# A third token buffer, a second stacked buffer, norms in four pieces, a late merge inside a pair, and inverses by block transposes, in an attention-plus-FFN kernel on one Trainium2 core

## The reference

```python
x = x + attn(layernorm(x), ctx, mask)      # LN of x again inside attn, with g1, b1; LN of ctx with g2, b2
#   q = xn @ Wq.T; k = cn @ Wk.T; v = cn @ Wv.T      (16 heads of 32)
#   softmax(q k^T / sqrt(32), masked) @ v, then @ Wo.T + bo
x = x + ffn(layernorm(x))                   # ffn: rows and weight quantised to fp6 (e2m3) with a
#   scale per block of 32, then xd @ wd.T + bias
```

## Time and profile before

| what | value |
|---|---|
| three runs | 4701.99, 4707.31, 4712.32 us, median 4707.31 |
| the profiled execution | 4703.17 us, span 4701.4 us |
| mean granted TensorE clock | 0.992 |
| busy share | PE 94%, DVE 76%, POOL 63%, ACT 60% |
| transfers | 532.38 MB, mean 113 GB/s |
| accumulating transfers (POOL's queue) | 318.79 MB |

### The profile page before, as it was taken

The page is one execution under the profiler, slowest core; times in us unless marked ns, Lnnn a source line. Parts: engine busy times, 40 slices in busy tenths (PEclk is TensorE's granted clock), DMA queues, the critical chain, the costliest instruction groups (busy, mean ns, idle before and its releaser), DMA issues.

```text
span 4701.4 us, 89975 instructions
## 1 busy us (share of the span) xinstructions
PE 4416.6 (94%) x37008; PEld 1505.2 (32%) x37008; DVE 3550.8 (76%) x3943; ACT 2830.0 (60%) x5128; POOL 2975.3 (63%) x1818
## 2 busy tenths in 40 slices
PE   4999889999899999999989999899989999899998
PEld 2322243222432224322342223422234222342223
DVE  4689667886588965889658986589965898658985
ACT  3387734776347864477545875458744577446773
POOL 2188742887438874388734887348873588625886
PEclk9999999999999999999999999999999999999999
DMA  5255642656326563356533555335554355543553
GB/s 192 56 119 112 140 136 57 122 110 164 106 59 123 115 163 103 70 110 122 154 107 73 109 118 155 104 78 119 112 146 111 79 118 110 143 112 74 119 113 98
DMA packets 190014, 532.38 MB, mean 113 GB/s; under 512 B 28625, under 2 KB 102673, under 8 KB 148386
## 3 DMA queue, kind: packets, MB, share of 16 engines
q0 software_dynamic: 43776, 318.79, 33.7%
q1 hardware_dynamic: 145826, 207.83, 14.5%
HBM read 110.98 MB, written 21.01 MB: 28 GB/s over the span
## 4 chain that ended last, share of the span: by engine, by line
PE 48%; POOL 15%; DVE 11%; DMA 7%; issue 6%; ACT 6%; SPq 6%; DVEq 0%; ACTq 0%; POOLq 0%
PE banks L963 12%; PE banks L975 12%; PE banks L878 10%; POOL wkT_wvT_wqT L412 9%; PE banks L937 8%; DMA wdT<-wkT_wvT_wqT 6%; SPq L297 5%; ACT region L757 4%; DVE max_parts L596 4%; PE banks L1001 3%; POOL sums L412 2%; POOL wdT L412 1%; PE banks L847 1%; DVE amax L544 1%; DVE x_stats L511 1%
## 5 line engine op out<-in xcount | busy, mean ns | idle before, releaser
L596 DVE TENSOR_REDUCE max_parts<-banks 128x2 f32<-128x1024 f32 x2048 | 2400.6, 1218 | 384.0 <-PE banks L937 367.9
L757 ACT ACTIVATE region<-banks 128x512 f32<-128x512 f32 x4096 | 2208.4, 597 | 585.0 <-PE banks L963 442.4
L412 POOL TENSOR_TENSOR wkT_wvT_wqT<-region 128x1024 f32<-128x1024 f32 x608 | 1522.9, 2744 | 455.8 <-ACT region L757 455.2
L963 PE MATMUL banks<-queries_stacked,keys_stacked 98*32 98x512 f16 x16384 | 1363.3, 384 | 97.0 <-ACT region L757 73.1
L975 PE MATMUL banks<-region,values 128*32 128x512 f32 x8192 | 1075.5, 599 | 19.9 <-ACT region L757 7.7
L963 PEld LDWEIGHTS banks<-queries_stacked,keys_stacked 98*32 98x32 f16 x16384 | 415.1, 94 | 1322.6 <-ACT region L757 1036.1
L937 PE MATMUL banks<-keys_stacked,queries_stacked 33*128 33x512 f16 x4096 | 697.6, 385 | 7.3 <-DVE max_parts L596 3.5
L878 PE MATMUL banks<-region,wkT_wvT_wqT 128*128 128x512 f16 x2304 | 569.9, 385 | 58.8 <-DVE region L587 45.0
L614 DVE RECIPROCAL row_sums_inverse<-row_sums_inverse 128x128 f32<-128x128 f32 x256 | 232.1, 930 | 259.3 <-ACT row_sums_inverse L774 259.3
L412 POOL TENSOR_TENSOR sums<-region 128x1024 f32<-128x1024 f32 x160 | 405.8, 2750 | 0.8 <-ACT region L757 0.2
L393 POOL TENSOR_TENSOR region<-row_sums_inverse,region 128x512 f16<-128x512 f32 x80 | 92.5, 1156 | 491.4 <-ACT region L732 491.4
(11 more groups left out here) (83 smaller groups left out, 3304.0 us busy)
## 6 DMA issues: line engine op xcount, KB each, us to landing
wdT<-wkT_wvT_wqT POOLq DMA_DIRECT2D x96, 1024.0 KB, 11.9
wkT_wvT_wqT<-wkT_wvT_wqT POOLq DMA_DIRECT2D x80, 1024.0 KB, 7.6
sums<-wkT_wvT_wqT POOLq DMA_DIRECT2D x72, 1024.0 KB, 7.6
keys_stacked<-region SPq DMA_DIRECT2D x768, 64.0 KB, 2.0
wkT_wvT_wqT<-sums POOLq DMA_DIRECT2D x40, 1024.0 KB, 7.6
region<-in_x SPq DMA_DIRECT2D x24, 1024.0 KB, 7.9
wkT_wvT_wqT<-weights_split SPq DMA_DIRECT2D x8, 3072.0 KB, 18.3
queries_stacked<-region SPq DMA_DIRECT2D x384, 64.0 KB, 2.0
```

The costliest lines, as they stand in the source:

```text
L412: e.tensor_tensor(SUMS[dst][:, half], PR[i][:, half], PR[i + 1][:, half], ALU.add).then_inc(s_pr, 1)
L596: e.tensor_reduce(mpart[:, buf, :, a, t, c], MXB[parity], AX.X, ALU.max).then_inc(s_mxd, 1)
L757: e.activation(PR[u % 4][:, j * HALF:j * HALF + HALF], score_bank(kt, j)[0], ACT.Exp, scale=SCALE).then_inc(s_ex, 1)
L963: mm = e.matmul(dst[HD * t:HD * t + HD, :], KA[0:STR, ds(ka + (j * C + (u + 1) * P + HD * t), HD)], QA[0:STR, ds(qa[j], HALF)], start=True ...
```

## The change

In the front there are three token buffers (the third over `V[:, 8 * D:12 * D]`), chosen by `chunk_tokens`, and chunk 2 is loaded in the tail of the batch before, behind the weights (for the first batch behind them at the start). Chunk 3 is loaded when chunk 0 is turned, chunk 4 when chunk 1 is, chunk 5 before `stack(2)`. `KS` has two buffers by the parity of the chunk, the second over `SUMS[3]`, and the semaphores of stacked rows are four. The norm of chunk `f + 2` goes through four pieces, one for each q/k contraction of chunk `f` (before: two, at i = 2 and at the next chunk's i = 0), and GpSimd's `rstd` comes after the first of four low parts instead of after the fourth.

In the units, the last late merge moves from behind pair 6 into pair 0 of the next unit, between its two halves. The inverse of row sums, which were four reciprocals of 128 columns, becomes a transpose in 32x32 blocks into a scratch tile, one reciprocal over column 0 of each of the 16 blocks (sums are equal along each head's 32 partitions), and a transpose back which reads that column 32 times. It stands behind the maxima of tiles 14 and 15 instead of those of tiles 14, 15, 0 and 1.

```diff
-        KS = R[:, 6144:8192].bitcast(F16).rearrange("p (s g t) -> p s g t", s=2, g=G)
+        XB = [... (R[:, 4096:6144], V[:, 12 * D:16 * D], V[:, 8 * D:12 * D])]
+        chunk_tokens = lambda c: XB[(0, 1, 2, 0, 1, 0)[c]]
+        KS = [t.bitcast(F16).rearrange("p (s g t) -> p s g t", s=2, g=G) for t in (R[:, 6144:8192], SUMS[3])]
-        s_kd = [sem(f"stacked_rows_stored{i}") for i in range(2)]
+        s_kd = [[sem(f"stacked_rows_stored{i}_{h}") for h in range(2)] for i in range(2)]
@@ SyncE
             projection_weights()
+            tokens(XCH, context_chunks(0)[:, 0])
             for b in range(0, B):
+                def context_tokens(c, turned):
+                    e.wait_ge(s_tp, b * (CC * NCH) + CC * (turned + 1))
+                    tokens(c, context_chunks(b)[:, c - XCH])
...
+                context_tokens(3, 0)
                 for par in range(2):
                     e.dma_start(KA[MASK[par]:MASK[par] + 1, :]...
-                def context_tokens(c):
-                    if c < NCH:
-                        e.wait_ge(s_tp, b * (CC * NCH) + CC * (c - 1))
-                        tokens(c % 2, cb[:, c - XCH])
-                context_tokens(2)
                 for c in range(NCH):
-                    context_tokens(c + 3)
+                    if c == 0:
+                        context_tokens(4, 1)
+                    if c == 2:
+                        context_tokens(5, 3)
                     stack(c)
...
                     projection_weights()
+                    tokens(XCH, context_chunks(b + 1)[:, 0])
@@ GpSimd
-                def low_tokens(b, c, full):
+                def low_tokens(b, c, full, call=None):
                     for cc in range(CC):
...
+                        if cc == 0 and call:
+                            rstd(call)
-                        def pair(p, dst):
+                        def pair(p, dst, halfway=None):
...
+                                if h == 0 and halfway:
+                                    halfway()
+                        def merge_last():
+                            e.wait_ge(s_ac2, (late - 1) * 16)
+                            src = buffers(2 * g + q - 1)[2]
+                            e.wait_ge(s_pr, n * 14 + 2)
+                            e.dma_start(SUMS[second], SUMS[src], accum_op=ALU.add).then_inc(s_ac2, 16)
-                        pair(0, first)
-                        if g + q > 0:
-                            e.wait_ge(s_ac2, (late - 1) * 16)
+                        pair(0, first, merge_last if g + q > 0 else None)
                         pair(1, one)
...
                         if not end:
-                            merge_late(0, 5, one)
+                            merge_late(5, one)
                         pair(6, two)
-                        if not end:
-                            merge_late(1, 6, two)
@@ VectorE
             def norm_stats(tiles, stats, mean_var, var, twice=False):
...
-                    if twice and i == 1:
+                    if i == 1:
                         yield
@@ norm: the same for the four centrings
-                    def invert(m, t):
-                        if t == 0:
-                            e.wait_ge(s_on, m + 2)
-                        part = RL[:, t * P:t * P + P]
-                        inv = e.reciprocal(part, part)
-                        if t == QT - 1:
-                            inv.then_inc(s_inv, 1)
+                    def invert_first(m):
+                        e.wait_ge(s_on, m + 2)
+                        ch.did(e.transpose(TF[1], RL[:, :]))
+                        ch.settle()
+                        ch.did(e.reciprocal(sums_turned[:, :, 0], sums_turned[:, :, 0]))
+                    def invert_rest():
+                        ch.settle()
+                        e.transpose(RL[:, :].rearrange("p (k e) -> p k e", e=HD),
+                                    sums_turned[:, :, 0:1].broadcast_to([P, HALF // HD, HD])).then_inc(s_inv, 1)
...
                             max_row(idx + 24 + 2 * t, q, 3 * QT + t)
-                            if n > 0 and t >= 2:
-                                invert(m - 1, t - 2)
+                            if n > 0 and t == 2:
+                                invert_first(m - 1)
+                            if n > 0 and t == 3:
+                                invert_rest()
                         for t in range(QT):
                             max_row(idx + 32 + 2 * t, q, t)
-                            if n > 0 and t < 2:
-                                invert(m - 1, t + 2)
...
                     if p == "qk" and i == 0:
-                        next(parts, None)
-                    if p == "qk" and i == 2:
                         parts = iter(())
                         if f + 2 < NCH:
                             parts = norm(f + 2, b, b * CALLS + (CALLS_FIRST + f + 3 - XCH))
+                    if p == "qk":
                         next(parts, None)
@@ ScalarE
                 def high_part(f, i, j):
-                    if f > 0 and i % 2 == 0:
-                        e.wait_ge(s_kd[i // 2], (b * NCH + f) * (16 * 3 * J))
+                    if f > 1 and i % 2 == 0:
+                        e.wait_ge(s_kd[f % 2][i // 2], (b * NCH // 2 + f // 2) * (16 * 3 * J))
```

More of the change, by code:

```diff
@@ L119, in build @@
         T4 = [split(R[:, 2048 * i:2048 * i + 2048]) for i in range(2)]
-        XB = [t.rearrange("p (n d) -> p n d", n=4) for t in (R[:, 4096:6144], V[:, 12 * D:16 * D])]
-        KS = R[:, 6144:8192].bitcast(F16).rearrange("p (s g t) -> p s g t", s=2, g=G)
+        XB = [t.rearrange("p (n d) -> p n d", n=4) for t in (R[:, 4096:6144], V[:, 12 * D:16 * D], V[:, 8 * D:12 * D])]
+        chunk_tokens = lambda c: XB[(0, 1, 2, 0, 1, 0)[c]]
         PR = [R[:, 2048 * i:2048 * i + 2048] for i in range(4)]
@@ L193, in build @@
         s_mk = sem("mask_row_loaded")
-        s_x = [sem(f"tokens_loaded{i}") for i in range(2)]
+        s_x = [sem(f"tokens_loaded{i}") for i in range(3)]
         s_ve = sem("variance_ready")
@@ L296, in stack @@
                                 dst = KAv[rows, gs, j, k0:k0 + HALF] if c >= XCH else QAv[rows, gs, c, j, :]
-                                e.dma_start(dst, KS[HD * j:HD * j + HD, part, gs, :]).then_inc(s_kd[h], 16)
+                                e.dma_start(dst, KS[c % 2][HD * j:HD * j + HD, part, gs, :]).then_inc(s_kd[c % 2][h], 16)
                 KAv = KA[:, :].rearrange("p (g j t) -> p g j t", g=G, j=J)
                 QAv = QA[:, :].rearrange("p (g q j t) -> p g q j t", g=G, q=2, j=J)
+                context_tokens(3, 0)
                 for par in range(2):
@@ L353, in _ @@
             e.wait_ge(s_out[1], B * 64 + 16)
-            for c in range(2):
-                e.wait_ge(s_x[c], B * NCH // 2 * 16)
+            for c in range(3):
+                e.wait_ge(s_x[c], B * NCH // 3 * 16)
             e.wait_ge(s_wr, B * 16)
@@ L394, in low_tokens @@
                                         ALU.subtract).then_inc(s_tl, 1)
+                        if cc == 0 and call:
+                            rstd(call)
                 if b == 0:
                     low_tokens(0, 0, TF_FIRST)
-                for c in range(NCH):
-                    if c > 0:
-                        low_tokens(b, c, TF)
-                    if XCH <= c + 1 < NCH:
-                        rstd(b * CALLS + (CALLS_FIRST + c + 2 - XCH))
+                for c in range(1, NCH):
+                    low_tokens(b, c, TF, b * CALLS + (CALLS_FIRST + c + 2 - XCH) if c + 1 < NCH else None)
                 for g in range(0, G):
@@ L423, in merge, with merge_late @@
                             e.dma_start(SUMS[first], SUMS[src], accum_op=ALU.add).then_inc(s_acc, 16)
-                        def merge_late(i, p, src):
+                        def merge_late(p, src):
                             e.wait_ge(s_pr, n * 14 + 2 + 2 * (p + 1))
-                            if i > 0:
-                                e.wait_ge(s_ac2, (late + i) * 16)
+                            e.dma_start(SUMS[second], SUMS[src], accum_op=ALU.add).then_inc(s_ac2, 16)
[3 more added lines that the diff above has]
+                            e.wait_ge(s_pr, n * 14 + 2)
                             e.dma_start(SUMS[second], SUMS[src], accum_op=ALU.add).then_inc(s_ac2, 16)
@@ L528, in norm @@
             def norm(c, b, call):
-                tiles = [XB[c % 2][:, i, :] for i in range(4)]
+                tiles = [chunk_tokens(c)[:, i, :] for i in range(4)]
                 twice = c < XCH
-                e.wait_ge(s_x[c % 2], b * (8 * NCH) + c // 2 * 16 + 16)
+                e.wait_ge(s_x[c % 3], b * (NCH // 3 * 16) + c // 3 * 16 + 16)
                 yield from norm_stats(tiles, stats, mv, ve[:, :], twice)
@@ L628, in unit @@
                     if last:
-                        for t in range(QT):
-                            invert(m - 1, t)
+                        invert_first(m - 1)
+                        invert_rest()
```

(19 more changed lines are left out.)

11 lines of the change are left out of this document (6 added, 5 removed).

## The result

| | before, on the same chip | changed |
|---|---|---|
| median of 4 runs each | 4706.96 us (4701.99 to 4712.32) | 4581.14 us (4573.34 to 4583.54) |
| profiled execution, span | 4703.17, 4701.4 us | 4573.34, 4571.5 us |
| mean granted TensorE clock | 0.992 | 0.997 |

The ratio is 0.973, 95% interval 0.9713 to 0.9746. The forecast was 4571, its range 4535 to 4630. The spans of the two profiled executions differ by 129.9 us against a sum of 132; the medians differ by 125.8, since the profiled execution of the changed kernel is the fastest of its four, 7.8 us under their median. Even 129.9 is near 132 partly by luck, as the stages show. In the changed kernel low parts are line 597, high parts 754, maximum products 952, exponentials 771, `pair` 418, the last merge 442, statistics 521, centrings 536, the transposes 625 and 631.

What follows compares the result with a forecast made beforehand. TensorE alone sets middle units; losses lie in starved fronts and stretched last units. Gains 8.0 + 2.05 + 5.5 + 1.2 = 16.75 a batch, times eight 134.0, less 2: 4703 - 132 = 4571 us, 8-in-10 range 4535 to 4630.

Steps and rivals of the forecast that it cites:

- Front, 8.0 a batch: Stretch to the first maximum product: second stacked buffer removes stalls, 8 us a batch gained, bounds 4 and 9.8.
- 1 to 2 us of the 9.8 come back as a wait: Front's end: first maximum product needs stack(3)'s first half at 1300.9, against 1299.4 unstalled; 9.8 is the most obtainable.
- Rival 1: Front: SyncE's stack transfers, 16.75 against 12.1 us a chunk, set the pace; front returns 4 a batch, 4603 us; chance 0.14.
- Units 1 to 5, 2.05: Between first and sixth output copies: moved merge brings GpSimd's period below TensorE's 44.80 us; gain 2.05 a batch, lower bound 1.
- Rival 2: Units: the merge wait only moves; last two units give 2, units 1 to 5 give 1; 4607 us; chance 0.14.
- Last two units, 5.5: End of a batch, GpSimd taken as the bound: 90.2 us falls to 84.7, gain 5.5 a batch, bounds 2 and 7.5.
- half a unit 22.4: Last two units: half a unit of 22.4 us plus tiles without maximum products, together 84.0 us, TensorE and ScalarE's limit.
- Tail, 1.2: Tail: transposes and short reciprocal take 1.85 us for 3.39; gain 1.2 a batch, bounds 0 and 1.5.
- Cover of 4.6 us in a unit: Units: the two transposes cost nothing until together they pass 4.6 us, when TensorE needs the next reduction.
- Rival 3: Units: transposes wait for GpSimd's adds, 9.35 us each; 5135 us, or 4835 with one-pair blocks; chance 0.05.
- Start, -2: Kernel start: third token buffer's load shares transfers with weights TensorE awaits; loss 0 to 4 us once, 2 taken.
- Rival 5: Whole kernel: all caps reached, 9.8 + 2.05 + 7.5 + 1.5 = 20.9 a batch, 4536 us; chance 0.10.

Runs made afterwards that it cites:

- the run with four: The changed kernel with each transpose of the inverse done four times in units 1 to 5 of each batch: 4717.48 us, ratio 1.0018.
- the run with 362.19: The changed kernel with the norm in two pieces and rstd behind the fourth low part, three token buffers and early loads kept: 4582.77 us, ratio 0.973.
- with seven: The changed kernel with each transpose of the inverse done seven times in units 1 to 5 of each batch: 4930.23 us, ratio 1.0469.

## Why the prediction came out as it did

**Front, 8.0 a batch, measured 9.3.** The mechanism was right, and five of eight batches take 69.88 to 69.89 us, the 69.9 of the forecast's count of contractions and transposes. The step that failed is "1 to 2 us of the 9.8 come back as a wait" for `stack(3)`. SyncE got through three stacks and a token load in 48.61 us (1201.57 to 1250.18), not 3 x 16.75 + 1.3 = 51.6, so the twelfth transfer of the fourth was issued at 1257.2 and landed at 1259.2, 2.7 us before the product at 1261.96. Rival 1 (4 a batch) therefore fell: SyncE is behind, and stays within the slack that the values give. (Its 4 is also low by its own figures: 9.8 less 4.65 is 5.2, and 4 comes out only with the wait of 1 to 2 us taken off as well.) The pieces of the norm, costed at nothing, were worth 1.2 a batch; the forecast asked what they might cost and not what the block of 3.5 us already cost. Without them the front would have returned 8.1, the 8 of the forecast for another reason. The wait for tokens came (83.1 us of VectorE's time) and was free in the fronts of 69.9 us.

**Centrings beside GpSimd.** A pair of centrings alone takes 0.99 us; a pair beside low tokens 2.27 and 2.21:

```profile
1200.26 2.27 DVE L536 TENSOR_SCALAR values<-values,mean_var,rstd 128x512 f32<-128x512 f32 x2
...
1203.72 0.99 DVE L536 TENSOR_SCALAR values<-values,mean_var,rstd 128x512 f32<-128x512 f32 x2
```

The Trainium skill ("SBUF — State Buffer", Who interferes with whom) has this exclusion, and the trace agrees: a pair beside low tokens took 1.2 to 1.3 us more, about one low-token subtraction of 1.16. The profile does not show in which mode a centring ran. The slack of the contraction hid it whole, since TensorE did not stop once in this front; so the price of 2 a batch that the rule would have set on the front was not paid.

**Units 1 to 5, 2.05, measured 1.88.** Right: output copies stand 44.79 to 44.80 us apart, but for six of the 40, 44.98 to 45.09, which the runs did not explain. Rival 2 (the wait only moves) fell. GpSimd's wait was forecast before the last merge at 2 to 5 us. It is gone there, and 4 to 5 us before pair 0 instead, because GpSimd no longer carries a lag.

**Last two units, 5.5, measured 3.6.** This term was mis-sized, and the failed step is "half a unit 22.4". The last unit took 41.74 us against 41.6. The one before it took 44.71 to 44.83 against 42.4. Its copy was at 1596.69, and its tile 8 begins, by ScalarE's rows, 27.05 us later; from there to the next copy it is 17.78 us, about 2.5 a tile as forecast.

```profile
1623.74 2.06 ACT L771 ACTIVATE region<-banks 128x512 f32<-128x512 f32 x4 [0.22 <-PE banks L978]
...
1629.07 2.06 ACT L771 ACTIVATE region<-banks 128x512 f32<-128x512 f32 x4 [0.40 <-PE banks L978]
```

In those 27.05 us TensorE is busy for 27.00: the first half of this unit holds all of its maximum products and most of the former unit's row sums, so it is no half of 44.8. Half a unit of 27.05 and 7 tiles, for 22.4 and 8 tiles, is the 2.4 us by which the unit came out longer. GpSimd, which the forecast called the bound, had stopped being it.

**Tail, 1.2.** Right, with its upper bound 1.5 and the out-projection late next. A transpose takes 703 to 705 ns in the mean of 64 and 715 at most, against 0.7 taken. The estimate of 0.53 from the Trainium skill ("Vector Engine (DVE) Microarchitecture Reference", The reshape front-end and per-opcode configuration) was short by 0.17, unless all of that is start-up, which no run here separates.

**Cover of 4.6 us in a unit.** Wrong, and without effect on the time, since the changed kernel's two stops take 1.6: it is 2.8 for both together. Rival 3 fell because the transposes never waited for GpSimd, as the Trainium skill ("SBUF — State Buffer", Who interferes with whom) says of one-input instructions, while the two-input scaling beside them still takes 6.47 us in the mean of 24. But the rival's point of decision, 8 us for both transposes together, stood too high. With the measured cover it is 16.75 / 5 + 2.8 = 6.2, and in the run with four, where the stops are 6.0, the whole gain of the change is gone (1.0018).

**Start, -2, measured +1.2.** The load shared with the weights stopped nothing. In the five kernels without the early load the start takes 66.1 to 66.6 us, in the nine with it 65.1 to 65.5. So the early load helps even there; no run shows why.

The sum was near because 10.7 us too little in the front and 3.2 at the start stand against 15 too much in the last two units: that is luck. Rival 5 had the front's cap nearly right (9.8, measured 9.3), and the last two units' wrong.

## What to carry to other kernels

Before pricing the removal of a stall, count what the engine that sets the stage still has to do in that very stretch, row by row; an average (half of a unit) missed a stretch of 27 us by 4.6 where the front's count met 69.9 us to 0.1. A block of work longer than one step of the pipeline that it stands beside is a stall already, even if each of its instructions is short, so look for gain in splitting it. Read small parts in their own stage: two parts worth 9 to 10 us each, taken back, were invisible in the medians and plain in the stage sums. And where a lowered clock and a wait stand in the same stretch, compare it with the same stretch at full clock before charging time to the clock.

## What the runs showed of the hardware

**The clock falls at joins, and there it costs time.** Between the last contraction of a front and the first output copy the same work takes 45.0 us in one batch and 46.2 in another; in other runs 48.5, and once 50.1. The two windows below are the second and the third batch of the changed kernel, with their granted clock.

```profile
764.09:809.09 45.00, 42.57 (x468) 12.38 (x466) 36.82 (x33) 36.65 (x68) 36.38 (x18) 1.00 0.40 80
1326.23:1372.42 46.19, 43.95 (x468) 12.58 (x466) 36.81 (x33) 36.65 (x68) 36.41 (x18) 0.96 0.39 78
```

The fall comes a few us into the second window, after slices in which TensorE waited for the first exponentials:

```profile
1326.00:1328.00 2.00, 1.11 (x9) 0.31 (x11) 1.95 (x2) 0.60 (x1) 0.00 (x0) 1.00 0.01 1
1328.00:1330.00 2.00, 1.35 (x17) 0.33 (x16) 0.00 (x0) 1.46 (x3) 0.00 (x0) 1.00 0.00 0
1330.00:1332.00 2.00, 1.83 (x14) 0.48 (x17) 0.00 (x0) 1.71 (x4) 0.00 (x0) 0.51 0.00 0
1332.00:1334.00 2.00, 2.00 (x20) 0.43 (x12) 0.00 (x0) 0.52 (x2) 1.74 (x1) 0.64 0.00 0
```

Summed over eight joins this stretch took between 362.19 and 374.81 us in the kernels here, though none of the edits touches it: 12.6 us, a third more than one of the small parts is worth. The fall shows in two of eight joins of the run with 362.19, in six of the changed kernel (367.21), and in seven of the run with 374.81, the inverse alone. What decides whether it comes is open.

**Elsewhere a lowered clock can be free.** In the units of the run with four transposes a unit with a mean clock of 0.96 took the same 47.98 us as one at 1.00, because VectorE set the time. So the mean clock of a run (0.985 with four, 0.964 with seven) does not say how much time was lost to it.
